# Two of four tiles of layer 0's output transposed by DMA in 16-bit halves instead of by TensorE

## What is computed

```
# layer 0: 16 heads of 64, masked, softmax over keys, bias everywhere
attn = exp(einsum(qh, kh) * mask - max) * mask;  attn /= sum + 1e-15
y    = layernorm(attn @ vh @ Wo + bo + x) * gamma + beta
# layer 1: 16 heads of 32, query is y, keys and values from the context
q    = y @ Wq1.T;  p = softmax(q @ k1.T / sqrt(32))
out  = layernorm(y + (p @ v1) @ Wo1.T + bo1) * gamma1 + beta1
```

## Time and profile before

| | |
|---|---|
| median of 3 runs | 851.07 us (849.96 to 851.61) |
| the profiled execution, its own time | 850.99 us |
| its span, first to last instruction | 849.2 us |
| mean granted TensorE clock | 0.995 |
| busy in the span | PE 98%, DVE 67%, POOL 53%, ACT 47% |

### The profile page before, as it was taken

How to read it: one execution, slowest core, us unless ns; L and a number is a source line. 1 busy time by engine, 2 the same in 40 slices (tenths; PEclk the granted TensorE clock), 3 DMA queues, 4 the chain that set the end, 5 groups by cost and what they waited for, 6 DMA issues and landing times.

```text
span 849.2 us, 12709 instructions
## 1 busy us (share of the span) xinstructions
PE 829.6 (98%) x4652; PEld 561.8 (66%) x4652; DVE 569.9 (67%) x1307; ACT 403.1 (47%) x535; POOL 448.8 (53%) x285
## 2 busy tenths in 40 slices
PE   9999999999999999898999999999999999999996
PEld 6777475665657484385667577677676775776744
DVE  3567766767667585876766766747657567667587
ACT  4416373645546454733543634444536436354262
POOL 2022403123040405235878789689687886894446
PEclk9999999999999999998999999999999999999999
DMA  9518525161625044887360531433424515311002
GB/s 309 204 46 297 191 101 214 50 223 54 251 64 200 29 186 177 226 314 191 96 170 26 167 107 51 149 99 98 151 75 112 162 37 163 100 50 51 1 26 74
DMA packets 50429, 112.37 MB, mean 132 GB/s; under 512 B 4544, under 2 KB 10944, under 8 KB 50368
## 3 DMA queue, kind: packets, MB, share of 16 engines
q1 hardware_dynamic: 49408, 111.23, 40.3%
q10 hardware_dynamic: 960, 0.34, 0.2%
HBM read 77.47 MB, written 34.08 MB: 131 GB/s over the span
## 4 chain that ended last, share of the span: by engine, by line
PE 68%; POOL 12%; DVE 8%; issue 5%; DMA 3%; ACT 3%; SPq 1%; DVEq 0%; POOLq 0%; ACTq 0%
PE bank L501 15%; PE bank L502 15%; PE bank L503 14%; PE bank L557 7%; PE bank L533 6%; POOL a_raw L1585 4%; POOL a_lo L1590 4%; PE bank L540 3%; POOL a_lo L1596 3%; PE bank L695 3%; DVE scores L1304 2%; DMA r_bc<-r_dram 2%; ACT a_hi L968 1%; DMA wk_sb<-wk 1%; PE bank L667 1%
## 5 line engine op out<-in xcount | busy, mean ns | idle before, releaser
L1548 POOL TENSOR_TENSOR x_lo<-x_raw,x_hi 128x2048 fp32r<-128x2048 f32 (+1 forms) x8 | 35.6, 4448 | 196.3 <-ACT x_hi L873 180.7
L501 PE MATMUL bank<-wo_lo,a_hi 128*128 128x512 f32 x320 | 127.7, 399 | 0.0
L502 PE MATMUL bank<-wo_hi,a_lo 128*128 128x512 f32 x320 | 124.8, 390 | 0.0
L503 PE MATMUL bank<-wo_hi,a_hi 128*128 128x512 f32 x320 | 124.7, 390 | 0.0
L1159 DVE CUSTOM_DVE_ANT_0 scores<-bank,mask_f 128x512 f32<-128x512 f32 x128 | 80.8, 687 | 51.9 <-PE bank L533 51.9
L1590 POOL TENSOR_TENSOR a_lo<-a_raw,a_hi 128x1024 fp32r<-128x1024 f32 x32 | 77.4, 2421 | 50.9 <-ACT a_hi L968 50.9
L501 PE MATMUL bank<-x_lo,wq_hi 128*128 128x512 f32 x256 | 101.1, 395 | 0.5 <-DVE q_lo L1148 0.5
L988 ACT ACTIVATE scores<-scores,sh 128x512 f32<-128x512 f32 x128 | 80.3, 710 | 41.0 <-DVE sh L1329 41.0
L502 PE MATMUL bank<-x_hi,wq_lo 128*128 128x512 f32 x256 | 99.7, 390 | 0.0
L503 PE MATMUL bank<-x_hi,wq_hi 128*128 128x512 f32 x256 | 99.7, 389 | 0.0
L885 ACT ACTIVATE q_hi<-bank,bq_sb 128x512 fp32r<-128x512 f32 x64 | 44.1, 690 | 100.9 <-PE bank L503 97.3
(11 more groups left out here) (179 smaller groups left out, 1668.1 us busy)
## 6 DMA issues: line engine op xcount, KB each, us to landing
u_dram<-u_out SPq DMA_DIRECT2D x8, 2048.0 KB, 7.3
a_raw<-u_dram SPq DMA_DIRECT2D x32, 512.0 KB, 3.7
r_bc<-r_dram SPq DMA_DIRECT2D x56, 256.0 KB, 5.0
x_raw<-x_t SPq DMA_DIRECT2D x8, 1024.0 KB, 5.6
xn<-x_n SPq DMA_DIRECT2D x8, 1024.0 KB, 5.3
xb_dram<-xn SPq DMA_DIRECT2D x8, 1024.0 KB, 5.8
z<-xb_dram SPq DMA_DIRECT2D x32, 256.0 KB, 2.9
out<-z SPq DMA_DIRECT2D x6, 1024.0 KB, 7.3
```

What stands on the lines that cost most here:

```text
L501: nc.tensor.matmul(dst, lh, rl, start=first, stop=False)
L502: nc.tensor.matmul(dst, ll, rh, start=False, stop=False)
L503: return nc.tensor.matmul(dst, lh, rh, start=False, stop=last)
```

## The change

Tiles 0 and 1 of each block (TURNED = 2) are no longer transposed by TensorE. For each of the two:

- ScalarE writes the 16-bit halves of the normalized rows apart into `halves` (`split`), directly after `normal0` of that tile;
- SyncE issues a transposing DMA of the 128 x 1024 16-bit values into `halves_t` (`turn`), SBUF to SBUF, after `load_r(i+1, 1)` and ahead of `store_out(i-2)` (in block 0 ahead of `store_r(2..7)`);
- ScalarE puts the halves together again into `yt_raw` (`join`), and `yt_high` reads `yt_raw` instead of a PSUM bank; both joins stand ahead of `normal0(i, 2)`;
- GpSimd makes the low part (`yt_low`), after `scales0(i, 1)`, in place of VectorE; in block 0 ahead of `attention0(1, 0)`.

`yt_raw` lies on `yt_lo`, the halves on `q1_hi`, so `split` also waits for the logits of block i-1 (in block 0 for `attention_first`), and `q1_high(i, 0)` for both joins. With it orders move: `output1(i-1, 0)` follows `output0(i, 3)` directly; on GpSimd the four `a1_low` come ahead of `a0_low(i+1, 1)`, which goes behind the new `yt_low`; on ScalarE `a1_high` comes ahead of `a0_high(i+1, 1)`, `a0_high(i+1, 2)` and `(i+1, 3)` come later, `q1_high(i, 3)` ahead of `normal1`; `scales1` goes ahead of `resid_bias(i, 0)`; in block 7, 6 of the 12 matmuls of `output1(6, 1)` go ahead of `transposes(7, 2)`, and 6 of the 12 of `output1(6, 2)`, which all stood behind `logits1(7, 2)`, go ahead of `queries1(7, 0)`. VectorE keeps `yt_low` of tiles 2 and 3. The counts of the semaphores follow.

```diff
@@ -102,6 +105,7 @@
                lambda k: (put(k, "yt_hi yt_lo", [P, KC, QB], f32r), put(k, "q1_hi q1_lo", [P, C1, QB], f32r)),
+               lambda k: (skip(k, 8), put(k, "yt_raw", [P, KC, QB]), put(k, "halves halves_t", [P, TURNED, 2 * D], u16)),
                lambda k: (skip(k, 16), put(k, "r_first", [P, QT, TW])))
@@ -390,9 +396,18 @@
                 if i > 0:
-                    sp.wait_ge(yt_psum_ready, QT * (i - 1) + n + 1)
+                    if n < TURNED:
+                        sp.wait_ge(split_ready, TURNED * (i - 1) + n + 1)
+                    else:
+                        sp.wait_ge(yt_psum_ready, (QT - TURNED) * (i - 1) + n - TURNED + 1)
                     sp.wait_ge(rg_ready, 2 * (i - 1) + n // 2 + 1)
                 sp.dma_start(z0[:, n, :], xb_dram[i, n]).then_inc(xb_loaded[n], 16)
+            def turn(i, n):
+                sp.wait_ge(split_ready, TURNED * i + n + 1)
+                sp.dma_start(halves_t[:, n, :].rearrange("p (g q) -> p g q", g=2 * KC), halves[:, n, :],
+                             transpose=True).then_inc(turn_loaded[n], 16)
@@ -451,6 +466,8 @@
                         load_r(i + 1, n)
+                for n in range(TURNED):
+                    turn(i, n)
                 if i == 0:
@@ -669,7 +684,8 @@
             def queries1(i, c):
-                pe.wait_ge(yt_ready, QT * (i + 1))
+                pe.wait_ge(yt_ready, (QT - TURNED) * (i + 1))
+                pe.wait_ge(turned_low_ready, TURNED * (i + 1))
                 if c >= 2:
@@ -791,23 +809,21 @@
                 output0(i, 3)
-                transposes(i, 0)
-                transposes(i, 1)
                 if i == 0:
...
                     output1(i - 1, 0)
-                if before and i < NB - 1:
-                    output1(i - 1, 1)
+                    output1(i - 1, 1, 0, C1 if i < NB - 1 else C1 // 2)
                 transposes(i, 2)
...
                 if i == NB - 1:
-                    output1(i - 1, 1)
+                    output1(i - 1, 1, C1 // 2)
+                    output1(i - 1, 2, 0, 2)
                 elif before:
@@ -825,7 +841,7 @@
             i = NB - 1
-            output1(i - 1, 2)
+            output1(i - 1, 2, 2)
             logits1(i, 3)
@@ -972,13 +988,38 @@
+            def split(i, n):
+                act.wait_ge(n0_ready, QT * i + n + 1)
+                if i > 0:
+                    act.wait_ge(logits1_ready, H1 * i)
+                else:
+                    act.wait_ge(attn0_ready, QT)
+                nc.scalar.activation(halves[:, n, :].rearrange("p (h f) -> p h f", h=2),
+                                     z0[:, n, :].bitcast(u16).rearrange("p (f h) -> p h f", h=2),
+                                     ACT.Copy).then_inc(split_ready, 1)
+            def join(i, n):
+                act.wait_ge(turn_loaded[n], 16 * (i + 1))
+                nc.scalar.activation(yt_raw[:, :, qcols(n)].bitcast(u16).rearrange("p c (q h) -> p h c q", h=2),
+                                     halves_t[:, n, :].rearrange("p (h c q) -> p h c q", h=2, c=KC),
+                                     ACT.Copy).then_inc(joined_ready, 1)
             def yt_high(i, n):
-                act.wait_ge(yt_psum_ready, QT * i + n + 1)
-                nc.scalar.activation(yt_hi[:, :, qcols(n)], TQ_BANKS[n % 2][:].rearrange("p (c q) -> p c q", c=KC),
-                                     ACT.Copy).then_inc(yt_hi_ready, 1)
+                if n < TURNED:
+                    act.wait_ge(joined_ready, TURNED * i + n + 1)
+                    turned_rows = yt_raw[:, :, qcols(n)]
+                else:
+                    act.wait_ge(yt_psum_ready, (QT - TURNED) * i + n - TURNED + 1)
+                    turned_rows = TQ_BANKS[n % 2][:].rearrange("p (c q) -> p c q", c=KC)
+                nc.scalar.activation(yt_hi[:, :, qcols(n)], turned_rows, ACT.Copy).then_inc(yt_hi_ready, 1)
...
                 act.wait_ge(q1_psum_ready, C1 * i + c + 1)
+                if c == 0:
+                    act.wait_ge(joined_ready, TURNED * (i + 1))
                 nc.scalar.activation(q1_hi[:, c, :], TQ_BANKS[c % 2][:], ACT.Identity,
@@ -1030,26 +1071,28 @@
                 normal0(i, 0)
+                split(i, 0)
                 normal0(i, 1)
+                split(i, 1)
                 if before:
...
                         a0_high(i + 1, 0)
+                    for c in range(C1):
+                        a1_high(i - 1, c)
                     if more:
                         a0_high(i + 1, 1)
-                    for c in range(C1):
-                        a1_high(i - 1, c)
+                join(i, 0)
                 yt_high(i, 0)
+                join(i, 1)
                 yt_high(i, 1)
...
                 normal0(i, 3)
-                if before and more:
-                    a0_high(i + 1, 2)
                 yt_high(i, 2)
...
                 if before and more:
-                    a0_high(i + 1, 3)
+                    a0_high(i + 1, 2)
                 if i == 0:
@@ -1057,16 +1100,18 @@
                 q1_high(i, 0)
+                if before and more:
+                    a0_high(i + 1, 3)
                 q1_high(i, 1)
...
                 q1_high(i, 2)
+                if not before:
+                    a0_high(1, 3)
+                q1_high(i, 3)
                 if before:
...
                     normal1(i - 1, 1)
-                else:
-                    a0_high(1, 3)
-                q1_high(i, 3)
                 if before and more:
@@ -1427,8 +1473,6 @@
                 moments0(i, 3)
-                yt_low(i, 0)
-                yt_low(i, 1)
                 if i == 0:
@@ -1612,6 +1656,12 @@
+            def yt_low(i, n):
+                pool.wait_ge(yt_hi_ready, QT * i + n + 1)
+                nc.gpsimd.tensor_tensor(yt_lo[:, :, qcols(n)], yt_raw[:, :, qcols(n)], f(yt_hi[:, :, qcols(n)]),
+                                        ALU.subtract).then_inc(turned_low_ready, 1)
             def scales1(i, first=0, last=QT):
@@ -1692,24 +1742,32 @@
                     scales0(i, 1)
+                    for n in range(TURNED):
+                        yt_low(i, n)
                 if more:
-                    for n in (0, 1):
-                        attention0(i + 1, n)
-                        a0_low(i + 1, n)
+                    attention0(i + 1, 0)
+                    a0_low(i + 1, 0)
+                    attention0(i + 1, 1)
+                    if not before:
+                        a0_low(i + 1, 1)
                 if before:
...
                     scales0(i, 1)
+                    for n in range(TURNED):
+                        yt_low(i, n)
+                    if more:
+                        a0_low(i + 1, 1)
                 if more:
...
                 resid_scale(i, 0)
-                resid_bias(i, 0)
                 if before and more:
...
                     scales1(i - 1, 0, 2)
+                resid_bias(i, 0)
                 resid_scale(i, 1)
```

More of the change, by code:

```diff
@@ L31, in cross_attention_program @@
                             sum_sel, identity, out):
-    f32, f32r, i32 = mybir.dt.float32, mybir.dt.float32r, mybir.dt.int32
+    f32, f32r, i32, u16 = mybir.dt.float32, mybir.dt.float32r, mybir.dt.int32, mybir.dt.uint16
     ALU, ACT, AX = mybir.AluOpType, mybir.ActivationFunctionType, mybir.AxisListType
@@ L46, in ends_of @@
             return MAX_ENDS if i < NB - 1 else LAST_ENDS
+        TURNED = 2
         def sb(stack, name, shape, dt=f32):
@@ L138, in cross_attention_program @@
         a1_hi, a1_lo, a1_raw, a1_last, s_stage = named("a1_hi a1_lo a1_raw a1_last s_stage")
-        q0_hi, q0_lo, yt_hi, yt_lo, q1_hi, q1_lo, r_first = named(
-            "q0_hi q0_lo yt_hi yt_lo q1_hi q1_lo r_first")
+        q0_hi, q0_lo, yt_hi, yt_lo, q1_hi, q1_lo, r_first, yt_raw, halves, halves_t = named(
+            "q0_hi q0_lo yt_hi yt_lo q1_hi q1_lo r_first yt_raw halves halves_t")
         k0_hi, k0_lo, x_hi, x_lo, a_lo, a_hi, a_raw, wo_stage, a1_early_hi, a1_early_lo = named(
@@ L238, in cross_attention_program @@
         rg_ready, resid_ready = sems("rg_ready resid_ready")
+        split_ready, joined_ready, turned_low_ready = sems("split_ready joined_ready turned_low_ready")
+        turn_loaded = [sem(f"turn_loaded{n}") for n in range(TURNED)]
         yt_psum_ready, yt_hi_ready, yt_ready, q1_psum_ready, q1_hi_ready, q1_ready = sems(
@@ L657, in transposes @@
             def transposes(i, n):
-                if n >= 2:
-                    pe.wait_ge(yt_ready, QT * i + n - 1)
-                elif i > 0:
-                    pe.wait_ge(*((q1_ready, C1 * i) if n == 0 else (turned1_ready, i)))
+                if i > 0:
+                    pe.wait_ge(*((q1_ready, C1 * i) if n % 2 == 0 else (turned1_ready, i)))
                 else:
@@ L745, in output_last, with output1 @@
                 last.then_inc(o1_ready, 1)
-            def output1(i, n):
+            def output1(i, n, first=0, last=C1):
                 if i == 0 and n == 0:
@@ L763, in output1 @@
```

(25 more changed lines are left out.)

## The result

The changed kernel takes 853.62 us (median of 12 runs, 852.29 to 855.06) and the kernel before 851.14 in runs beside it: a ratio of 1.0027 [1.0016, 1.0038], by which it is 2.3 us slower (the brackets are a 95% interval, here and below). The prediction was 852.4. The profiled execution took 852.29 us, the lowest of the 12; its span is 850.5, its mean granted clock 0.992.

What follows compares the result with a forecast made beforehand. TensorE, busy 98% of the span, was taken as the bound. Gains of 8.2 us in blocks 1 to 6 and 0.4 in block 7 against 10.0 lost in block 0 gave +1.4 on 850.99: 852.4 us, range 846 to 870.

Steps and rivals of the forecast that it cites:

- The balance: Whole kernel: 8.2 us gained in blocks 1 to 6, most of it paid back once by 10.0 in block 0.
- The gain of a block, 1.36: Blocks 1 to 6: 0.79 us of removed transposes plus 0.57 of closed wait, 8.2 us over six blocks.
- the hole of the earlier trace: `output1(2, 0)` in block 3: TensorE loses 0.57 us a block to GpSimd's `a1_low`; to close with about 1 us to spare.
- TensorE's list has no other hole: Blocks 1 to 6: used to exclude, but for a small rest, that removing the transposes gains nothing.
- A turn's cost: Each transposing transfer: 2 us of SyncE's queue and 4 us from issue to landing.
- The limit on X: X, SyncE's queue time per turn: free up to 4.4 us, beyond it 2 us a block for each us.
- at another rate than 1.06: Sign of being wrong: ScalarE's 16-bit copies of 1024 elements not taking the assumed 1.06 us.
- GpSimd's slack: Blocks 1 to 6: GpSimd's wait for the moments falls from 5.4 us to about 1.
- Block 0: Turns land at 392.5 and 394.5, `queries1(0, 0)` 11.6 late, less 2.65 idle, plus 1 for late logits: loss 10.0 us.
- block 0 pays half: Rival, chance 0.20: block 0's turns overtake the loads, landing at 387.4 and 389; 5.4 us less loss, 847.0.
- this cancels: Block 0: the lower clock after the old idle time returns after the new, longer wait, so no net effect.
- Block 7: `queries1(7, 0)` about 0.4 us earlier, the six matmuls taken from later standing before logits that wait anyway: gain 0.4.

Runs made afterwards that it cites:

- experiment 2: Changed kernel with block 0's four tiles all transposed by TensorE, blocks 1 to 7 keeping the turns: 841.67 us, ratio 0.9890 to the kernel before.
- Experiment 8: Kernel before, no turns, GpSimd's four `a1_low` ahead of `a0_low(i+1, 1)` and ScalarE's `a0_high(i+1, 2)` and `(i+1, 3)` later: 845.26 us, ratio 0.9932.
- Experiment 4: Kernel before, no turns, with GpSimd's four `a1_low` ahead of `a0_low(i+1, 1)` and ScalarE's `a1_high` ahead of `a0_high(i+1, 1)`: 855.18 us, ratio 1.0044.
- experiment 5: Changed kernel with SyncE waiting for each turn's landing in blocks 1 to 7, holding the queue 3.1 us a turn: 853.47 us, ratio 1.0030.
- experiment 6: Changed kernel with each turn done twice and each waited for in blocks 1 to 7, 6.2 us of queue a tile: 867.12 us, ratio 1.0181.
- Experiment 7: Changed kernel with turns doubled and waited for in blocks 1 to 7, and the 1 MB store issued ahead of them: 858.20 us, ratio 1.0073.
- experiment 3: Changed kernel with block 0's two turns issued ahead of block 1's first loads: 845.67 us, ratio 0.9942 to the kernel before.
- experiment 1: Changed kernel with all twelve matmuls of `output1(6, 2)` back behind `logits1(7, 2)` in block 7: 852.31 us, ratio 1.0012 to the kernel before.

## Why the prediction was near, point by point

- **The balance** (a gain in six blocks, paid back in block 0): right, and shown by experiment 2, where the gain stands alone. That the total came so close is partly luck: the gain was put 2.5 us too low (8.2 for 10.7), the loss of block 0 0.6 too low (10.0 for 10.6), and block 7 was forecast at -0.4 and measured at +1.55, so that errors of 2.5 one way and 2.6 the other cancel.
- **The gain of a block, 1.36.** Measured 1.78. The mechanism is right (the hole of the earlier trace rows closed, the transposes gone), the size is short, also without block 1, in blocks 2 to 6 with 1.70. Experiment 8 splits it: the orders give 0.87, not 0.57, mostly since the stop at `queries1` goes too and block 1 gains more than the others; the turning gives 0.91, not 0.79, as the slower first matmuls behind the transposes go with them. "TensorE's list has no other hole" overlooked the second hole of experiment 8: the first matmul of `queries1` took 0.50 and the next one 0.34 to follow, the mark of a short stop that the timeline prints without a wait.
- **Where the gain comes from.** The prediction gave the hole's closing to GpSimd's order, and ScalarE's later copies stand only in the description of the change. Experiment 4 shows that half of the order loses 4.0 us, and experiment 8 that both halves gain 5.9.
- **A turn's cost.** I took 2 us of queue and 4 to land; measured 1.24 and 3.1, under both, near the plain load of the earlier trace rows. The estimate of 10.5 us from the Trainium skill (VectorE: DVE Perf Modes, The three transpose paths) does not hold here: eight 128 x 128 pieces land after 3.1 us, so pieces don't run one behind the other at 1309 ns. The estimate of 1.0 us from the Trainium skill (DMA: Bandwidth & Descriptors, Latency and other measured facts) is worked out from a rate alone; the landing after 3.1 us may hold more than the bytes' own time, as the 2.9 of the plain load of the same bytes may, and no run here separates the two.
- **The limit on X.** Free at 3.1 (experiment 5), as said. At 6.2 I had 2 us a block for each us over 4.4, that is 3.6 a block; experiment 6 gave 1.7 to 2.8. The wait that I named is there (4.65 us of VectorE for the store), but it cost TensorE only 1.3 us in block 3, and the rest came from loads behind the store, which I had not priced. Experiment 7 shows that in blocks 2 to 6 it is the store's place that costs, not the turns' time; in block 1 the late second join costs.
- **ScalarE.** The split is 1.06 as taken; the join is 1.37, so one of the signs of being wrong ("at another rate than 1.06") came true for the joins. It cost nothing in the middle blocks, since `normal0(3, 2)` behind the joins still waits for GpSimd for 2.04 us.
- **GpSimd's slack**, 5.4 to about 1: measured 0.80.
- **Block 0.** Landings of 392.5 and 394.5 were forecast, 391.3 and at most 393.2 measured (ScalarE stood at the first join and not at the second); experiment 3 shows the place behind the loads as the cause of 8.0 of the 12.0 us. That stands against "block 0 pays half". The stretching of the logits, put at 1 us, was larger, some 4 us: from the first logits to the mark it is 24.0 us before and 25.4 after, though 2.8 us are gone that the lower clock cost before. So against the stretch stands the clock, where "this cancels" failed. Windows of the changed kernel (length, busy us of the engines, granted clock, DMA share, GB/s):

```profile
388.00:389.00 1.00, 0.00 (x0) 0.00 (x0) 0.00 (x0) 0.00 (x0) 0.00 (x0) 0.96 0.97 219
389.00:390.00 1.00, 0.00 (x0) 0.00 (x0) 0.00 (x0) 0.00 (x0) 0.00 (x0) 0.50 1.29 176
...
398.00:400.00 2.00, 2.00 (x4) 0.83 (x4) 1.18 (x2) 1.65 (x2) 0.85 (x1) 0.71 0.00 0
400.00:405.00 5.00, 5.00 (x19) 3.30 (x18) 2.86 (x3) 2.14 (x2) 4.72 (x2) 1.00 0.02 3
```

  Most of the stretch at the lower level passes while TensorE has nothing to do; it costs the transposes and the values product some 1.2 us (1.73 and 3.72 from start to start, against 1.17 and 3.04), and from 400 to 405 the clock is 1.00, where the earlier trace rows have 0.56. The first logits and the twelve matmuls behind them take 3.8 us from 407.48, where they took 6.6 before. So the clock gives back 2.8 and costs 1.2, a net 1.6 of the 4 that the stretched logits lose.
- **Block 7** is the step that failed: "`queries1(7, 0)` comes about 0.4 earlier." It comes at the same time, 26.49 us behind block 6's mark for 26.47 before, since the six matmuls of `output1(6, 2)` put ahead of it fill the place of the six of `output1(6, 1)` that went forward. "The six matmuls taken from later stand in front of logits that wait for VectorE's score copies anyway" is true of those logits (43.79 and 43.77), but it means that there the six were free, and in front of the queries they are not: experiment 1 gives 1.3 us in the times and 1.1 in block 7 where the clock stays up. Instead of a gain of 0.4 block 7 changes by nothing at the full clock and by +1.55 with the drop. That `normal0(7, 2)` holds the transposes came true (0.22 of idle time).
- **Not named** was the lateness of block 1's loads of tiles 2 and 3 (GpSimd waits 5.43 us for them, 3.83 before), which follows TensorE's by way of VectorE's reciprocals and the stores. No run undid it alone, so its share of the 10.6 is open.

## What to carry to other kernels

When work leaves the engine that sets the pace, price the first and last passes of the loop by themselves: the cover that makes a transfer free in the middle is missing there, and here they took back all that six blocks gave. Before an edit is credited with closing a hole, run the reorderings that come with it alone: here they gained 5.9 us by themselves where the whole change lost 2.3, and half of them lost 4.0. Work that stands in front of an instruction which waits anyway costs nothing there; moved to where nothing waits, it costs time.

## What the runs showed of the hardware that was not expected

- A transposing transfer SBUF to SBUF of 128 x 1024 values of 16 bits held the queue for 1.24 us and landed after 3.1; nobody waited for 15 of the 16. The two of block 0, behind 2 MB of loads, held the queue for 6.04 together and landed after up to 8.1.
- ScalarE's copy of 128 x 1024 values of 16 bits took 1.06 us reading with a stride and writing in a row, and 1.37 reading in a row and writing with a stride.
- A wait of 1.29 us on TensorE near the end was followed by the lower level of the clock (0.50 over the 2 us from 815.82) in the changed kernel's profile, by a like drop in those of experiments 2, 6 and 7, and by the full clock in those of experiments 3 and 5, with the same wait (1.27 to 1.30). What decides it was not found.
